# A head laid out anew, an order of their own for the first eight iterations, and another task order on all engines for the rest

## What is computed

```python
x = x + layernorm(attn(layernorm(x), Wq, Wk, Wv, Wp, bp, rel_table))
x = x + layernorm(ffn(layernorm(x), W_r, W_k, W_v, mu_r, mu_k))

# attn: scores = q @ k.T * scale + bias[clip(j - i)], causal, softmax, @ v, @ Wp + bp
# ffn:  xr, xk = mixes of each token with the one before it
#       sigmoid(xr @ W_r) * (square(relu(xk @ W_k)) @ W_v)
```

## Time and profile before

| what | us |
|---|---|
| median of 3 runs | 2209.36 (2208.81 to 2209.72) |
| the profiled execution's own time | 2206.79 |
| its span, first to last instruction | 2204.5 |
| PE / DVE / ACT / POOL busy in the span | 2068.1 / 1947.6 / 1757.1 / 1798.8 |
| first 83.4 us (head and n = -2, -1): PE busy | 30.6 |

### The profile page before, as it was taken

The page is one execution under the profiler, slowest core; times in us unless marked ns, Lnnn a source line. Parts: engine busy times, 40 slices in busy tenths (PEclk is TensorE's granted clock), DMA queues, the critical chain, the costliest instruction groups (busy, mean ns, idle before and its releaser), DMA issues. The chain is left out here.

```text
span 2204.5 us, 76383 instructions
## 1 busy us (share of the span) xinstructions
PE 2068.1 (94%) x29904; PEld 1390.0 (63%) x29904; DVE 1947.6 (88%) x5227; ACT 1757.1 (80%) x2644; POOL 1798.8 (82%) x1485
## 2 busy tenths in 40 slices
PE   2797999999999999999999999999999999999976
PEld 1354566666666666666667666666666666666655
DVE  8786878999999999999999999999999998898857
ACT  2577888888888888888888888888888888888844
POOL 4367767889898998898889889988888898888862
PEclk8898999999999999999999999999999999999988
DMA  7111212233223222322322333222322322221251
GB/s 177 35 45 30 50 36 71 60 74 79 62 60 68 70 65 72 79 72 53 74 62 67 69 79 76 58 64 62 73 67 75 79 55 58 56 66 55 67 125 41
DMA packets 337606, 147.99 MB, mean 67 GB/s; under 512 B 173024, under 2 KB 336480, under 8 KB 337248
## 3 DMA queue, kind: packets, MB, share of 16 engines
q1 hardware_dynamic: 337248, 143.11, 26.6%
HBM read 25.04 MB, written 43.06 MB: 31 GB/s over the span
## 5 line engine op out<-in xcount | busy, mean ns | idle before, releaser
L1837 POOL TENSOR_TENSOR probs<-probs_f,probs 128x1024 f16<-128x1024 f32 (+3 forms) x704 | 1116.4, 1601 | 185.5 <-ACT probs L1040 178.1
L1020 ACT ACTIVATE probs_f<-score_ps,score_unit 128x1024 f32<-128x1024 f32 (+3 forms) x704 | 619.9, 881 | 278.9 <-DVE score_ps L1361 125.3
L1343 DVE TENSOR_REDUCE row_max<-max_ps 128x2 f32<-128x1024 f32 (+2 forms) x640 | 629.6, 1001 | 11.0 <-PE max_ps L719 10.9
L1040 ACT CAST probs<-probs_f 128x1024 f16<-128x1024 f32 (+3 forms) x704 | 573.3, 814 | 18.4
L753 PE MATMUL misc<-v_pair,probs 128*128 128x65 f16 x4608 | 440.4, 194 | 1.7 <-issue 1.7
L754 PE MATMUL misc<-v_pair,probs 128*128 128x64 f16 x4608 | 439.2, 193 | 0.0
L755 PE MATMUL misc<-v_pair,probs 128*128 128x65 f16 x4608 | 438.4, 193 | 0.0
L753 PEld LDWEIGHTS misc<-v_pair,probs 128*128 128x128 f16 x4608 | 418.0, 97 | 28.0 <-issue 22.2
L754 PEld LDWEIGHTS misc<-v_pair,probs 128*128 128x128 f16 x4608 | 419.2, 98 | 0.9
L755 PEld LDWEIGHTS misc<-v_pair,probs 128*128 128x128 f16 x4608 | 419.2, 98 | 0.0
L640 PE MATMUL misc<-xT,w_split 128*128 128x512 f16 x1536 | 368.2, 383 | 21.0 <-DVE q_lo L1302 17.1
(11 more groups left out here) (201 smaller groups left out, 3827.3 us busy)
## 6 DMA issues: line engine op xcount, KB each, us to landing
v_pair<-v_calc SPq DMA_DIRECT2D x64, 516.0 KB, 3.9
o_scratch<-o_stage SPq DMA_DIRECT2D x128, 256.0 KB, 3.2
xh<-x SPq DMA_DIRECT2D x56, 128.0 KB, 3.2
x_res<-x SPq DMA_DIRECT2D x56, 128.0 KB, 2.6
out<-tail SPq DMA_DIRECT2D x56, 128.0 KB, 1.7
shift_all<-shift_row SPq DMA_DIRECT2D x256, 1.0 KB
probs<-wqkv SPq DMA_DIRECT2D x1, 3072.0 KB, 12.8
probs<-band_scratch SPq DMA_DIRECT2D x8, 144.0 KB, 6.4
```

The costliest lines, as they stand in the source:

```text
L1020: nc.scalar.activation(dst, score_ps[t % 2][:, :, 0:width], ACT.Exp, scale=score_unit[:]).then_inc(exp_done, 1)
L1040: nc.scalar.copy(dst, src).then_inc(hi_done, 1)
L1343: last = dve.tensor_reduce(dst[:, :, i % 4:i % 4 + 1], max_ps[:, :, col:col + width], AX.X, ALU.max)
L1837: pool.tensor_tensor(low, copy_of(par + ahead, t)[:, 0:2 * width], high, ALU.subtract).then_inc(lo_done_pool, 1)
```

## The change

Three things change. What is computed stays, but for the constant that masks a score (-2^100 in place of -3e38).

**Head.** The loads are issued as Wq, Wk, x in two halves, the bands, then Wv. The largest weight is found by a PE transpose, a DVE maximum, a diagonal and a matmul with ones (`turn_tops`, `row_tops`, `diag_tops`, `spread_tops`); no `partition_all_reduce` is left in the program. ACT normalises the first tokens and scales the bands in pieces, the piece of pair 0 first. Queries and keys of pair 0 are projected into the score banks as soon as half of the tokens are there; values come last. The nine fills of pair 0 rotate through three pairs of banks. The other 768 columns of the weights are scaled and split by ACT and POOL later on.

**First eight iterations.** n = -2 and -1 are written out; n = 0 to 7 run `early`, with an order of its own on each engine. The reductions for `wp` and the feed-forward weights are one (`late`, in n = 1), their splits are on ACT and POOL in n = 3 to 5.

**Iterations 8 to 63.** `body` has the same tasks as before in another order on all five engines.

Tasks and banks (the third number of a START entry is its bank):

```diff
-BANK = {name: bank for name, bank, _ in TASKS}
+EARLY_TASKS = [("o2", 1, "prev"), ("late", 0, "late"), ("o3", 0, "prev"), ("q0", 1, "qkv"), ("q1", 0, "qkv"),
+               ("o0", 1, "att"), ("v0", 0, "qkv"), ("k0", 1, "qkv"), ("v1", 1, "qkv"), ("o1", 0, "att"),
+               ("k1", 0, "qkv")]
+START = [("q0", -2, 2), ("k0", -2, 3), ("q1", -2, 4), ("k1", -2, 5), ("q0", -1, 0), ("q1", -1, 1), ("k0", -1, 0),
+         ("k1", -1, 1), ("v0", -2, 0), ("v1", -2, 1), ("v0", -1, 0), ("v1", -1, 1)]
...
+        fill_ps = [max_ps, score_ps[0], score_ps[1], max_ps, score_ps[0], score_ps[1], score_ps[0], score_ps[1], max_ps]
```

SP in the head:

```diff
-            sp.dma_start(x0, x_rows[0:NB].rearrange("g p c -> p g c")).then_inc(x0_in, 16)
-            sp.dma_start(w_f32, wqkv.rearrange("m (k p) n -> p m k n", p=P)).then_inc(weights_in, 16)
-            load_head(NB)
+            load_weights(0)
+            load_weights(1)
+            for half in range(2):
+                rows = slice(half * HALF, (half + 1) * HALF)
+                sp.dma_start(x0[:, rows], x_rows[rows].rearrange("g p c -> p g c")).then_inc(x0_in[half], 16)
...
-            for k in range(2):
-                sp.dma_start(wp_f32[k], wp[k * H * D // 2:(k + 1) * H * D // 2].rearrange("(k p) n -> p k n", p=P)
-                             ).then_inc(wp_in, 16)
-            held(band_out[0], 16)
+            load_weights(2)
+            load_head(NB)
+            held(band_out, 32)
```

PE in the head, q0 of pair 0 between the transposes, then the fills, values last:

```diff
+            project_qk("q0", -2, 0, 0)
+            transpose_heads(5)
+            transpose_heads(6)
+            project_qk("k0", -2, 0, 0)
...
+            first_fill(8)
+            score(-1, 1, 1, 0, -1)
+            transpose_maxima(1, -1)
+            project_v("v0", -2, 0, 0, 0)
+            project_v("v1", -2, 2, 0, 0)
+            project_v("v0", -1, 4, 0, 0)
+            project_v("v1", -1, 6, 0, 0)
```

PE, the end of `early`:

```diff
+                if has["next"]:
+                    fill(m, par, 7, at)
+                if has["att"]:
+                    weigh_values(1, m, par, 0)
+                    score(m, par, 0, 10, at)
+                if has["next"]:
+                    fill(m, par, 8, at)
+                if has["qkv"]:
+                    project_qk("k1", n, pair * P, ring)
+                if has["att"]:
+                    score(m, par, 0, 11, at)
+                if has["next"]:
+                    transpose_maxima(1, n)
+                    score(m, par, 1, 0, at)
```

ACT in the head:

```diff
+            scale_band(slice(0, 1))
+            high_part("q0", -1, 0, -2)
...
+            scale_bandT(slice(0, 2))
+            high_part("q0", -1, 1, -1)
+            shift(-1, 1, 1, 0)
+            split_rest(1)
+            high_part("q1", -1, 1, -1)
+            split_rest(0)
+            scale_band(slice(1, NPAIR))
+            high_part("k0", -1, 1, -1)
+            split_values()
...
+            split_rest(2)
+            scale_bandT(slice(2, H))
```

ACT, the start of `early`:

```diff
+                if n == LATE + 2:
+                    split_late()
+                if n == LATE + 3:
+                    split_ffn()
```

ACT, near the end of the new `body`:

```diff
+                if has["att"]:
+                    exponential(m, par, 0, 11)
+                    high_probs(m, par, 0, 11)
+                if has["next"]:
+                    exponential(m, par, 1, 0)
+                if has["mix"]:
+                    tail_gate(n)
```

DVE, the start of the new `body`:

```diff
+                if has["next"]:
+                    maxima(m, par, 1, 0)
+                if has["att"]:
+                    add_bias(m, par, 0, 1, at)
+                    low_probs(m, par, 0, 0)
+                if has["prev"]:
+                    outputs(2, m, par, 1)
+                    outputs(3, m, par, 1)
```

POOL in the head:

```diff
-            pool.wait_ge(top_ready, 1)
-            pool.partition_all_reduce(top_all[:], top[:], P, bass.bass_isa.ReduceOp.max).then_inc(top_reduced, 1)
-            pool.tensor_scalar(band_bf[:], band, band_unit[:, 0:1], MASKED, ALU.mult, ALU.max).then_inc(band_scaled, 1)
-            pool.tensor_scalar(bandT[:], bandT[:], band_unit[:, 0:1], MASKED, ALU.mult, ALU.max).then_inc(band_scaled, 1)
+            pool.tensor_scalar(w_f32[:, 0, :, FIRST:H * D], w_f32[:, 0, :, FIRST:H * D], w_scale[:, 0:1], None,
+                               ALU.mult).then_inc(q_scaled, 1)
+            rest_low(1)
+            rest_low(0)
```

More of the change, by code:

```diff
@@ L543, in _ @@
             held(cleared, 6)
[L544 to L569 removed]
+            load_shift(-1, 1, 1, 0)
@@ L571, in load_last @@
+            for n in range(N):
+                (early if n < NPAIR else body)(n)
             def load_last(j):
@@ L625, in transpose_heads, with turn_tops, spread_tops @@
                 last.then_inc(full["xt"], 1)
-            def project_qk(name, n, pair, ring, span):
+            def turn_tops(case, src, scratch):
+                count = src.shape[1]
+                pe.wait_ge(top_ready, case + 1)
+                pe.transpose(scratch[0:count, 0:P], src, ident[:]).then_inc(top_spread, 1)
+            def spread_tops(case, count, scratch):
+                pe.wait_ge(top_spread, 4 * case + 3)
+                pe.matmul(scratch[:, P:P + count], ones[0:count, :], top_diag[0:count, 0:count], start=True,
+                          stop=True).then_inc(top_spread, 1)
@@ L636, in project_qk @@
-                bank = opened(name, n, span)
+                if n == -LEAD:
+                    pe.wait_ge(split_lo, which + 1)
+                if n == 0:
+                    pe.wait_ge(split_lo, (4, 3)[which])
+                bank = opened(name, n)
                 step = 0
@@ L639, in project_qk @@
                     for w, a in ((0, 0), (1, 0), (0, 1)):
-                        last = pe.matmul(bank[:], w_split[:, w, which, k, bass.ds(pair, P)],
+                        last = pe.matmul(bank, w_split[:, w, which, k, bass.ds(pair, P)],
                                          xT[:, a, k, bass.ds(ring + half * 512, 512)],
@@ new lines, in _ @@
+            head_low(3, 3 * P, head_ps[3])
+            first_shift_unit()
+            for g in range(HALF, NB):
+                head_low(g, g * P, head_ps[g % 4])
+            low_part("q0", -1, 0, -2)
+            low_part("k0", -1, 0, -2)
+            low_part("q1", -1, 0, -2)
+            low_part("k1", -1, 0, -2)
+            maxima(-1, 1, 1, 0)
+            maxima(-1, 1, 1, 1)
+            maxima(-1, 1, 1, 2)
+            maxima(-1, 1, 1, 3)
+            find_top(2)
+            low_part("q0", -1, 1, -1)
```

1708 lines of the change are left out of this document (1061 added, 647 removed).

## The result

The changed kernel took **2160.2 us** (median of 4 runs, 2158.8 to 2161.7) beside 2209.5 us of the kernel before: a ratio of 0.978, 95% interval 0.976 to 0.979. The forecast was 2155 us, range 2134 to 2182. So the time came out 5 us above the forecast and inside the range. The single terms did not all come out: the head gave more than forecast, and the steady iterations lost time where a gain was forecast.

What follows compares the result with a forecast made beforehand. The head and iterations 1 to 7 were taken to wait, iterations 10 to 61 to be bound by PE. Savings of 20 + 25.5 + 1.5 + 8 = 55 from 2206.8 gave 2152, plus 2.6 for the median: 2155 us, range 2134 to 2182.

Steps and rivals of the forecast that it cites:

- the head: Start through iteration 0: bands at 32, pair 0's marker near 53 instead of 83.40; 20 us less, bounds 14 and 25.
- the steady iterations: Iterations 10 to 61: new order wins 0.15 us each of 0.24 us PE idle time, 8 us less.
- from it to the end of iteration 0 it was 28.1 us; left so: From iteration 0's first exponential to its end: the old 28.1 us kept, so the end moves from 114.59 to about 94.5.
- The lock: Head: only DVE instructions with two SBUF inputs contend with GpSimd, so maxima are unaffected and the 20 us stand, not 13.
- Iterations 1 to 7: Early iterations: 7 x 27.5 + 6 = 198.5 us against 224.14, 25.5 us less, bounds 11.6 and 31.
- the stall: Iteration 2: ACT's 11.6 us wait around POOL's feed-forward weight reduction goes entirely, as no POOL reduction is left.
- the weight work: Early iterations: extra ACT passes cost 2.5 and 2 us in iterations 3 and 4, DVE's joint reduction 1.5 in 1 and 2.
- Iterations 8 and 9: Iterations 8 and 9: PE's idle time ahead of the projection in the first of them goes, 1.5 us less.
- The direct wait on maxima: Iterations 10 to 61: PE waits 52 times at one fill, 9.1 us; most of this 0.17 per iteration goes.
- The rival "more headroom on PE": Steady part: waits hidden in PE's busy time can be won too, giving 25 to 30 us, about 2135 us; chance 0.08.
- The rival of DVE's outputs: Steady part: `outputs` 3 right behind `outputs` 2 delays tile 2's bias, cancelling the gain, 2209 to 2220 us; chance 0.05.
- The rival "brings nothing or costs a little": Steady order: PE waits as much elsewhere; 2163 us at zero gain, 2179 at 0.3 us lost per iteration; chance 0.17.

Runs made afterwards that it cites:

- run 8: The changed kernel with the early order ending after iteration 5, so iterations 6 and 7 take the steady order, on all five engines: 2168.8 us.
- Run 11: The kernel before, with one wait added so that GpSimd scales the bias bands only behind all six low parts of the weights: 2195.7 us.
- run 9: The changed kernel with one spare GpSimd reduction across partitions, its result read by nobody, added in iteration 6: 2175.7 us.
- Runs 6 and 7: The changed kernel with one spare 128-row matmul per iteration from 8 on, inside a 64-row stretch or beside 128-row work: 2175.4 and 2164.7 us.
- run 6: The changed kernel with one spare 128-row matmul per iteration from 8 on, between score tiles 4 and 5 inside a 64-row stretch: 2175.4 us.
- run 10: The kernel before, with one wait added so that GpSimd scales the bias bands only behind the first three low parts of the weights: 2208.1 us.
- run 1: The changed kernel again without any edit, on the chip of the next three runs: 2160.9 us.
- run 2: The changed kernel with the steady iterations back in the order of the kernel before on all five engines: 2157.2 us.

## Why the prediction came out as it did

- **The head: mechanism right, size off by 6.** Issue at 20.5 (18.4 forecast), but eight issues in 4.45 us, not 8.76, and the bands at 30.5, not 32. Four copies, nine maxima of 1.22, one search of 2.28: marker at 51.4 (53). First exponential at 64.9 (66). The recorded sum does not close: 34.3 and 16.3 make 50.6, and the 53 has 2.4 us without a term; the measured 51.4 lies nearer to the terms. The mis-sized term is the last, "from it to the end of iteration 0 it was 28.1 us; left so": it took 23.7. Iteration 0 also runs in the early order now, which the diff says, and I priced that order only from iteration 1 on. That this explains all of the 4.4 us is argued from iterations 6 and 7 (run 8, 3.9 us each), not tried for iteration 0.
- **The lock: held.** Maxima, which read PSUM, kept 1.22 us beside POOL. The 8.9 us of a split that the prediction names hold for two of the three; the first took 1.82. Run 11 adds how much of the old head the contention was: 9.8 of the 32.0 us at the marker, and 13 us of the time.
- **Iterations 1 to 7: 25.2 against 25.5, by parts that differ.** Iterations 5 to 7 take 27.55, 27.56 and 27.56 us, as forecast (27.5). Iteration 2 with the stall was 41.66 us before, 11.3 above the mean of the other six, 30.41 ((224.14 less 41.66) / 6), near the 11.6 of the forecast; run 9 prices it at 13.8 in the faster order. Iterations 1 to 4 take 30.95, 28.57, 28.59 and 28.15 us, so 3 and 4 lie 1.0 and 0.6 above 27.56, where 2.5 and 2 were put for the weight work, and 1 and 2 lie 4.4 above it, where 1.5 was put. Both sets sum to 6.0: the errors cancelled, which is luck. (The recorded range takes 16 as the lower end of this stage, where its own bound was 11.6.)
- **Iterations 8 and 9: not held.** The 2.1 us look like the 1.5 forecast, but come from the mark, as told under the ledger. The idle time of iteration 8 that was to go did not: it took 31.06 us after and 30.68 before. Nor do the last 143 us "keep their order": iterations 62 and 63 run in the new one.
- **The steady iterations: the step that failed** is "no more than the idle time can be won ... I take 0.15 each: 8 us", with the order assumed to touch nothing but idle time. A gain of the forecast's size did come: the 0.23 us by which the 45 earlier iterations stood above the last seven before (31.94 and 31.71) fell to 0.02, which is 9.6 us. The direct wait on maxima that the forecast named went too, but the wait of 0.20 us on ScalarE took its place. What was put at nothing is the order's own cost: 0.30 us in each of the 52, which is 15.8 us, and 9.6 less 15.8 is the measured -6.2. The new order cuts PE's 64-row work into eight stretches per iteration (fill 7 stands alone between the key projections and the second value projection) where the old one has seven. Runs 6 and 7 price a stretch at 0.21 us; 52 of them are 11 us. Of the other 0.09 us, 0.04 are idle time (1.37 us in the last seven after, 1.11 before); the rest has no price. No run put fill 7 back beside other 64-row work in the change itself, so its share there is inferred from the twins.
- **The rival "more headroom on PE"** fell: inside busy time 7.8 us were lost on balance. The premise was half right. Busy time does hide things, but here it hid mostly a cost of the new order. Its evidence is doubtful too: the 22.0 us are 0.42 us 52 times, and 0.42 us is also the gap of a weight load at a switch where nothing is waited for (run 6, 1332.87). The row of 21.6 us after the change is such a gap: in one iteration the load starts at 1020.90, and the DVE instruction that it names had ended at 1020.44. The Trainium skill's "Perfetto Trace Analysis", section "Identifying the Most-Contended Engine", warns of matmul busy share and trusts, beside the rate of useful work, the share of weight loads; that share went from 67% to 68% while the part grew slower, so on this kernel it pointed neither way.
- **The rival of DVE's outputs** fell too: DVE's wait for an output block, 16.9 us before, is not among its waits of 0.5 us and more after. The rival "brings nothing or costs a little" is what happened to this term, at 0.12 us per iteration.
- **The total: partly luck.** The head gave 6 us more than forecast and the steady iterations 14 less. That the time came within 5 us of the forecast is due to these errors offsetting each other, not to terms that were each right.

## What to carry to other kernels

When two orders of a PE-bound loop are compared, count the changes between matmuls of 64 and 128 rows as well as the waits: each change cost 0.1 us here, and the trace shows it as busy time, seen only in the distances between starts. When stages are compared by a mark, check that the mark has the same work on each side in both orders; the counts of matmuls tell. Keep DVE instructions with two SBUF operands apart in time from long GpSimd ones, even at the price of a wait; and do not call a reduction across partitions on GpSimd where it has a queue behind it. A loop whose order is set on five engines has no single task that may be moved alone: moving one small task by a place or two cost 20 and 35 us, and the old order on one engine alone 577 us.

## What the runs showed of the hardware

- In the rows of runs 6 and 7 a weight load starts ahead of its matmul when the matmul ahead has as many rows, not when 64 and 128 rows follow each other; two switches cost 0.21 us. The two 64-row matmuls of a pair run at the same time: in run 6 a pair of 512 columns starts at 1332.35, both within 0.01 us, and the next pair 0.21 us later. "TensorE: Matmul & The Clock Gate", section "The mechanism", of the Trainium skill says that a load overlaps running matmuls only when its row group differs from theirs. The 128-row load at 1324.51 beside a 128-row matmul speaks against that as it stands; the same section also lets a load for the background weight buffer go ahead, and that fits.
- A DVE instruction with two SBUF operands and a GpSimd instruction do not run beside each other: a split on DVE took 8.96 and 8.92 us in the kernel before and 1.81 in run 11. The scaling on GpSimd took 9.56 us in run 10, where it began 1.6 us before the end of such a split, and 8.07 in run 11. A maximum read from PSUM kept its 1.22 us beside GpSimd.
- A reduction across partitions held GpSimd for 5.5 us before and 7.1 us behind its own 0.4 (run 9), and 6.2 and 7.4 in the kernel before.
- The granted clock of iteration 1 differed between single executions of kernels with the same instructions up to there: 1.00 in the change (30.95 us), 0.95 in run 1 (32.50 us), 0.90 in run 2 (33.72 us). A mean between the levels of 2.4 and 1.2 GHz is meant. Ahead of it PE had stood still for 7.17 us in iteration 0. So 1.5 to 3 us of the difference between two such kernels is no effect of their edits.
